# First layer's hand-over from cross attention to the experts: the last batch in other PSUM banks, the next norm begun in the block before it, and the experts' weights for tiles 1 and 2 handled sooner

## The reference

```
def _L0_xattn_ref(hs, at, mask, Wq, bq, Wk, bk, Wv, bv, Wo, bo, ln_gamma, ln_beta, residual_scale):
    ...                                             # 16 heads of 16, over 256 keys
    scores = clip(einsum('bhsd,bhtd->bhst', q, k) / sqrt(16), -50, 50)
    probs = softmax(where(attend, scores, -50), axis=-1)
    ctx = einsum('bhst,bhtd->bhsd', probs, v)
    delta = clip(residual_scale, 0, 0.3) * (ctx @ Wo.T + bo)
    return layernorm(delta) * ln_gamma + ln_beta

def _moe_forward(x, router_weight, gate_up_proj, down_proj, sh_gate_w, sh_up_w, sh_down_w, shared_gate_w):
    shared = silu(x @ sh_gate_w.T) * (x @ sh_up_w.T) @ sh_down_w
    combine = top2_of_8(softmax(x @ router_weight.T))
    for e in range(8):
        gate, up = split(x @ gate_up_proj[e].T)
        out = out + (silu(gate) * up @ down_proj[e].T) * combine[:, e:e + 1]
    return out + sigmoid(x @ shared_gate_w.T) * shared

x = x + _L0_xattn_ref(_layernorm(x), ctx_2048, mask, ...)
x = x + _moe_forward(_layernorm(x), ...)
```

## Time and profile before

| | |
|---|---|
| median of 3 runs | 1137.29 us (1137.09 to 1137.39) |
| the profiled execution's own time | 1135.79 us |
| its span, first to last instruction | 1134.0 us |
| PE busy | 1014.3 us (89%), mean granted clock 0.959 |
| DVE busy | 748.9 us (66%) |
| ACT busy | 628.8 us (55%) |
| POOL busy | 402.7 us (36%) |
| DMA | 53.62 MB, mean 47 GB/s |
| the tail of the cross attention, from its last scores to the barrier | 421.9 to 444.8 us of the span |
| the experts' block up to the first matmul of tile 2 | 444.8 to 487.8 us |

### The profile page before, as it was taken

The page is one execution under the profiler, slowest core; times in us unless marked ns, Lnnn a source line. Parts: engine busy times, 40 slices in busy tenths (PEclk is TensorE's granted clock), DMA queues, the critical chain, the costliest instruction groups (busy, mean ns, idle before and its releaser), DMA issues. The chain is left out here.

```text
span 1134.0 us, 21031 instructions
## 1 busy us (share of the span) xinstructions
PE 1014.3 (89%) x7004; PEld 821.8 (72%) x7004; DVE 748.9 (66%) x2168; ACT 628.8 (55%) x1557; POOL 402.7 (36%) x381
## 2 busy tenths in 40 slices
PE   5799999999997984889998589999999997879978
PEld 4567777777764553778887368888888885767868
DVE  6667777777654576355655757777777775557984
ACT  2167777777773771233432557777777764334323
POOL 6466666666643012000000544443434331110150
PEclk9999999999999997799999699999999998988999
DMA  4250222111005000254441000001101000000111
GB/s 151 70 179 19 57 48 57 38 30 39 2 1 213 1 2 1 59 122 113 100 115 37 5 29 27 26 28 32 37 14 37 24 10 1 1 1 29 44 40 52
DMA packets 27242, 53.62 MB, mean 47 GB/s; under 512 B 4546, under 2 KB 11778, under 8 KB 26782
## 3 DMA queue, kind: packets, MB, share of 16 engines
q1 hardware_dynamic: 27166, 52.65, 16.9%
HBM read 42.56 MB, written 1.69 MB: 39 GB/s over the span
## 5 line engine op out<-in xcount | busy, mean ns | idle before, releaser
L387 POOL TENSOR_TENSOR sb_a_P<-sb_a_P,sb_a_rec 128x512 f32<-128x512 f32 x128 | 130.2, 1040 | 109.0 <-DVE sb_a_rec L592 109.0
L469 ACT ACTIVATE sb_a_P<-sb_a_nS,sb_a_nm 128x257 f32<-128x257 f32 x256 | 128.2, 508 | 19.7 <-DVE sb_a_nm L581 19.4
L581 DVE CUSTOM_DVE_ANT_0 sb_a_nS<-a_pS,sb_a_mask,sb_a_nsink 128x256 f32<-128x256 f32 x256 | 107.7, 480 | 42.1 <-PE a_pS L705 42.1
L478 ACT COPY sb_xn<-a_pT 128x512 f32<-128x512 f32 x128 | 74.9, 585 | 85.3 <-PE a_pT L719 84.6
L1785 ACT ACTIVATE sb_a_t<-a_pp,sb_a_w 64x512 f32<-64x512 f32 x128 | 87.4, 683 | 21.5 <-PE a_pp L142 17.1
L142 PE MATMUL a_pp<-sb_x_high,sb_a_w_low 128*128 128x512 f32 x188 | 83.4, 444 | 7.9 <-DVE sb_a_P L536 2.5
L719 PE MATMUL a_pT<-sb_ident,sb_a_P 128*128 128x128 f32 x512 | 82.0, 283 | 4.1 <-ACT sb_xn L478 4.1
L142 PE MATMUL a_pY<-sb_a_wo_high,sb_a_OT_low 128*128 128x256 f32 x256 | 74.7, 292 | 11.5 <-DVE sb_a_OT_low L135 9.4
L1858 DVE SCALAR_TENSOR_TENSOR sb_a_t<-a_pp,sb_a_w,sb_a_cs 128x512 f32<-128x512 f32 x64 | 47.8, 748 | 55.6 <-ACT sb_a_t L1785 55.5
L719 PEld LDWEIGHTS a_pT<-sb_ident,sb_a_P 128*128 128x128 f32 x512 | 55.3, 141 | 39.6 <-issue 32.4
L1716 POOL TENSOR_TENSOR sb_a_qT<-sb_a_t 128x512 f32<-128x512 f32 x32 | 41.1, 1286 | 117.4 <-DVE sb_a_t L1861 117.4
(11 more groups left out here) (374 smaller groups left out, 3056.7 us busy)
## 6 DMA issues: line engine op xcount, KB each, us to landing
sb_m_cw<-m_table SPq DMA_DIRECT2D x15, 512.0 KB
sb_a_kr<-sb_a_kall SPq DMA_DIRECT2D x56, 128.0 KB, 2.4
sb_f_w<-f_w SPq DMA_DIRECT2D x12, 384.0 KB, 3.1
sb_m_gu<-m_gu SPq DMA_DIRECT2D x17, 256.0 KB, 6.5
sb_a_w<-a_w SPq DMA_DIRECT2D x16, 257.0 KB, 2.7
sb_m_dn<-m_dn SPq DMA_DIRECT2D x17, 128.0 KB, 6.6
sb_a_w<-a_w SPq DMA_DIRECT2D x8, 259.0 KB, 2.6
sb_a_wo<-a_wo SPq DMA_DIRECT2D x8, 256.0 KB, 2.9
```

The costliest lines, as they stand in the source:

```text
L387: nc.gpsimd.tensor_tensor(part, part, rec[b % 2][:, h, :].rearrange("p (q o) -> p q o", o=1) .to_broadcast([P, 2, S]), ALU.mult).then_inc( ...
L469: out = nc.scalar.activation(Pm[b % 2][:, h, qt, 0:S + 1], nS[:, h, qt, 0:S + 1], ACT.Exp, bias=nm[b % 2][:, h, qt:qt + 1], scale=-1.0, ac ...
L478: nc.scalar.copy(PT[h], pT[:, :]).then_inc(PT_ready, 1)
L581: out = nc.vector.tensor_tensor_reduce(nS[:, h, qt, 0:S], pS[h][:, qt * S:(qt + 1) * S], wmask[:, qt, :], -1.0, nsink[par][:, h:h + 1], AL ...
```

## The change

Four things. (1) In the cross attention the last batch's tail uses banks of `pS`, which hold no more scores by then, in place of `pc`: its two halves have banks of their own, so that each half is transposed, copied and projected after its own semaphore (`turnedO`, `OT_ready`, `projected` count each half), and `turn_oT(3)` waits for the last exponential in place of `scaled`. (2) DVE does `add_normed(2)` at n = 37, behind `normalise(3, 0)` and `(3, 1)`. (3) The norm of the experts' input begins in the cross attention's block: DVE takes the statistics of tiles 0 to 3 at n = 28 and scales them at n = 31, with POOL's inverse root between `root(1)` and `root(2)`; the statistics of tiles 4 to 7 are DVE's last work before the barrier; in the experts' block POOL's root and DVE's scaling remain for the second half only. (4) In the experts' block ACT and DVE split the gate-up weights of tile 1 right behind the norm, in place of in step 0, and SP waits for the table inside its step, behind the request for gate-up weights.

```diff
@@ class BegunNorm
-        self.ln, self.rstd_ready, self.xn_ready = (k.sem(f"{tag}_{name}") for name in ("ln", "rstd_ready", "xn_ready"))
+        sem = lambda name: k.nc.alloc_semaphore(name=f"{tag}_{name}")
+        self.ln, self.rstd_ready, self.xn_ready = sem("ln"), sem("rstd_ready"), sem("xn_ready")
@@ cross_attention_0
+        following = k.norm_of_m0
+        LAST = B - 1
+        def bank_of_turned(b, qt):
+            return front[qt] if b == LAST else pc
+        def bank_of_O(b, qt):
+            return (front[2], pS[2][:, 0:NC])[qt] if b == LAST else pc
+        def bank_of_out(b, qt):
+            return half_of((front[3], pS[2][:, NC:2 * NC])[qt] if b == LAST else pc, qt)
@@ gpsimd
+            pool.sem_inc(following.rstd_ready, 1)
             for b in range(B):
                 root(b)
+                if b == 1:
+                    inverse_root(nc, pool, k, following.ln, following.rstd_ready, 0, halves=(0,))
@@ scalar, evac_OT
-                nc.scalar.copy(OT[:, :, :, :].rearrange("p t c q -> p (t c q)"), pc[:, :]).then_inc(OT_ready, 1)
+                if b < LAST:
+                    nc.scalar.copy(OT[:, :, :, :].rearrange("p t c q -> p (t c q)"), pc[:, :]).then_inc(OT_ready, 1)
+                    return
+                for qt in range(2):
+                    act.wait_ge(turnedO, b + 1 + qt)
+                    nc.scalar.copy(OT[:, qt, :, :].rearrange("p c q -> p (c q)"), half_of(bank_of_O(b, qt), qt)).then_inc(OT_ready, 1)
@@ vector
-                o = pc[:, :].rearrange("p (h n) -> p h n", h=X0_H)
+                o = bank_of_turned(b, qt)[:, :].rearrange("p (h n) -> p h n", h=X0_H)
...
-                    out = nc.vector.scalar_tensor_tensor(out=delta[:, 2 * b + qt, :], in0=half_of(pc, qt),
+                    if b == LAST:
+                        dve.wait_ge(projected, b + 1 + qt)
+                    out = nc.vector.scalar_tensor_tensor(out=delta[:, 2 * b + qt, :], in0=bank_of_out(b, qt),
...
-                    if n == 8 * b + 18:
+                    if n == 8 * b + 18 and b != LAST - 1 or n == 8 * b + 21 and b == LAST - 1:
                         add_normed(b)
+                if n == 28:
+                    dve.wait_ge(summed, HALF)
+                    row_stats(nc, dve, k, k.x, following.ln, 0, 0)
+                if n == 31:
+                    row_scale(nc, dve, k, k.x, k.xn, following.rstd_ready, 0, 0, following.xn_ready)
             dve.wait_ge(summed, NT)
+            row_stats(nc, dve, k, k.x, following.ln, 0, 1)
+            dve.wait_ge(following.ln, 4 * HALF)
@@ tensor, turn_oT
-                    else:
+                    elif b < LAST:
                         pe.wait_ge(scaled, b)
-                else:
+                    if b == LAST:
+                        pe.wait_ge(probs, X0_PAIRS)
+                elif b < LAST:
                     pe.wait_ge(O_ready, 2 * b + 1)
...
@@ tensor, turn_O and project_out
-                pe.wait_ge(O_ready, 2 * b + 2)
+                pe.wait_ge(O_ready, 2 * b + (1 if b == LAST else 2))
                 for qt in range(2):
+                    if b == LAST and qt == 1:
+                        pe.wait_ge(O_ready, 2 * b + 2)
...
+                    if b == LAST and qt == 0:
+                        out.then_inc(turnedO, 1)
                 out.then_inc(turnedO, 1)
...
+                    if b == LAST and qt == 1:
+                        pe.wait_ge(OT_ready, b + 2)
...
+                    if b == LAST and qt == 0:
+                        out.then_inc(projected, 1)
                 out.then_inc(projected, 1)
@@ experts_0
-            norm_and_turn(nc, k, ctx, "m0", [pg[0], pg[1], pu[0], pu[1]], split=True)
+            norm_and_turn(nc, k, ctx, "m0", [pg[0], pg[1], pu[0], pu[1]], split=True, begun=k.norm_of_m0)
@@ sync
                 sp.wait_ge(h_ready, 2 * n + 2)
+                sp.wait_ge(table_out, 16)
                 weights_of(n + 2, par)
...
-            sp.wait_ge(table_out, 16)
             with sp.Fori(0, PAIRS) as i:
@@ scalar
             gate_up_high(0, 0)
             on_scalar(act)
+            gate_up_high(1, 1)
             act.wait_ge(gates, 1)
...
-                if not (isinstance(n, int) and n == LAST):
+                if not (isinstance(n, int) and n in (0, LAST)):
                     gate_up_high(n + 1, 1 - par)
@@ vector
             gate_up_low(0, 0)
             lows_on_vector(dve)
+            gate_up_low(1, 1)
...
-                if not (isinstance(n, int) and n == LAST):
+                if not (isinstance(n, int) and n in (0, LAST)):
                     gate_up_low(n + 1, 1 - par)
@@ program
+        k.norm_of_m0 = BegunNorm(k, "m0")
         cross_attention_0(nc, k, src)
```

More of the change, by code:

```diff
@@ L1177, in turn_oT @@
                         pe.wait_ge(q_out, b + 3)
-                    else:
+                    elif b < LAST:
                         pe.wait_ge(scaled, b)
-                else:
+                    if b == LAST:
+                        pe.wait_ge(probs, X0_PAIRS)
+                elif b < LAST:
                     pe.wait_ge(O_ready, 2 * b + 1)
                 for q in range(X0_QUADS):
-                    out = nc.tensor.transpose(pc[:, q * P:(q + 1) * P],
+                    out = nc.tensor.transpose(bank_of_turned(b, qt)[:, q * P:(q + 1) * P],
                                               oT[q // 2][:, (q % 2) * S + qt * P:(q % 2) * S + (qt + 1) * P],
@@ L1188, in turn_O @@
             def turn_O(b):
-                pe.wait_ge(O_ready, 2 * b + 2)
+                pe.wait_ge(O_ready, 2 * b + (1 if b == LAST else 2))
                 for qt in range(2):
+                    if b == LAST and qt == 1:
+                        pe.wait_ge(O_ready, 2 * b + 2)
                     for c in range(KD):
-                        out = nc.tensor.transpose(pc[:, (2 * qt + c) * P:(2 * qt + c + 1) * P],
+                        out = nc.tensor.transpose(bank_of_O(b, qt)[:, (2 * qt + c) * P:(2 * qt + c + 1) * P],
                                                   O[qt][:, c * 8:(c + 1) * 8, :].rearrange("p h n -> p (h n)"),
                                                   k.tile["ident"][:, :])
+                    if b == LAST and qt == 0:
+                        out.then_inc(turnedO, 1)
                 out.then_inc(turnedO, 1)
@@ L1199, in project_out @@
                 for qt in range(2):
+                    if b == LAST and qt == 1:
+                        pe.wait_ge(OT_ready, b + 2)
                     for c in range(KD):
-                        out = nc.tensor.matmul(half_of(pc, qt), OT[:, qt, c, :], w[:, 3, c, :],
+                        out = nc.tensor.matmul(bank_of_out(b, qt), OT[:, qt, c, :], w[:, 3, c, :],
                                                start=(c == 0), stop=(c == KD - 1))
+                    if b == LAST and qt == 0:
+                        out.then_inc(projected, 1)
                 out.then_inc(projected, 1)
```

## The result

The changed kernel takes 1126.93 us (median of 7 runs, 1124.09 to 1131.36) beside 1137.29 us of the kernel before on the same chip (7 runs, 1136.42 to 1138.94): a ratio of 0.9911, 95% interval 0.989 to 0.9932. The prediction was 1128.2 us with a range of 1123.8 to 1131.8, and faster with a chance of 0.93. The profiled execution took 1124.25 us (before: 1135.79).

What follows compares the result with a forecast made beforehand. PE was taken as the bound, so only its waits or half-clock time pay: 6.7 (router) - 0.6 (clock) + 2.2 (request) + 0.8 (tile 2's clock) = 9.1 us, giving 1128.2 us, range 1123.8 to 1131.8.

Steps and rivals of the forecast that it cites:

- The tail: End of the cross attention, batch 3: its projection ends at 435.4 against 439.85, 4.45 us sooner.
- the case of full clock throughout: Batch 3's projection with no fall of PE's clock: ends at 434.5, router 7.6 us sooner.
- with the clock falling where it fell: Assumption for batch 3's projection: PE's clock falls at about 433.5 as before, so it ends at 435.4.
- The price of the half norm: Cross attention: statistics begun early delay PE's weighing by 0.15 us, bounds 0 and 1.7.
- The clock at the head: Experts' router and gate_up(0): the low-clock stretch may be up to twice 3.1 us; 0.6 us of loss taken.
- Tile 2's request: Experts' loop entry: tile 2's weights, requested right behind the table, land 2.2 us sooner, bounds 0.3 and 3.9.
- The rival of data that overtake the table: Tile 2's weights come in while the table is still being written: gain 12.3 us, 1125.0 us; chance 0.2.
- PE's idle time before tile 2: Sign in the experts' block: PE's idle time, 3.93 us before, would be under 3 us.
- the 0.8 us that I had credited to tile 2: Less idle time before tile 2 saves half of the 1.7 us lost there to PE's low clock.
- The hand-over alone: Rival: the request comes no sooner or the clock takes it back; gain 5.5 us, 1131.8 us; chance 0.13.
- the half norm on the path: Rival: clips move by 1.7 us, scalings by 1.35, projection at half clock; gain 5.2 us, 1132.1 us; chance 0.05.
- the slower loop: Rival: experts' loop tiles wait for data, at 1.0 us a tile over 14 tiles 1142.2 us; chance 0.03.

Runs made afterwards that it cites:

- the banks alone: The kernel before with only the last batch's own banks and the moved addition of batch 2: 1130.01 us beside 1137.75, ratio 0.9922.
- the addition back: The changed kernel with batch 2's addition again ahead of batch 3's divisions: 1129.11 us beside 1141.35, ratio 0.9903.
- the profile of after: First profiled execution of the changed kernel, set against the single profile of the kernel before: 1124.25 us beside 1135.79.
- the second profile: The unaltered changed kernel, timed and profiled again beside the version with early requests: 1128.25 us beside 1138.3 for the kernel before, ratio 0.9899.
- the request alone: The kernel before with only SP's table wait moved behind the gate-up request and tile 1's sooner split: 1136.53 us, ratio 0.9978.
- the wait back: The changed kernel with SP's wait for the table ahead of the experts' loop again: 1127.89 us, ratio 0.9884 to the kernel before.
- the kept-warm kernel: The changed kernel with tiles 2 and 3 requested at the experts' head, plus six and ten unused matmuls around the norm: 1122.65 us beside 1141.35, ratio 0.9835.
- with six: The kernel with early requests and unused matmuls, plus 6 of gate_up(0)'s matmuls between the router's: 1119.78 us beside 1138.3, ratio 0.982.
- with twelve: The kernel with early requests and unused matmuls, plus 12 of gate_up(0)'s matmuls between the router's: 1120.78 us, ratio 0.9841.

## Why the prediction was right

**The tail.** The working put the end of the projection at 435.4, the clock falling at 433.5; the case of full clock throughout was 434.5. In the profile the projection is taken up 20.20 us behind the landmark, or 434.46: the clock held, and the 7.6 us of that case are the 7.57 measured at the router. The step that was mis-sized is "with the clock falling where it fell". Before, PE waited 2.71, 0.81 and 0.67 us ahead of the last groups of the tail, and the clock fell at about 433.5; now the waits are 0.71, 0.78 and 0.18 us and the clock is at 1.00 up to 442. This is no chance of one execution: the projection took 1.99 us in all eleven profiles of kernels with the new banks, that of the banks alone (its end at 20.08) among them, and 3.78 us in all three with the old ones. One long wait is not what does it: with the addition back PE waits 2.27 us in one piece, and the clock holds. Which part of the old chain let it fall is open. The price of the half norm was 0.15 us predicted and some 0.1 measured.

**The clock at the head.** Predicted at +0.6 us, it was -1.5 in the profile of after and +1.1 in the second profile of the same kernel. The low stretch in `gate_up(0)`, 3.1 us before and allowed up to twice that, was 3.6 and 5.2 us. What the working did not have is that the router itself can begin at full clock, as it did in the profile of after. The guess was inside the spread by luck, and its sign is not a property of the change.

**Tile 2's request.** 2.2 us predicted; 2.36 in the change, 2.33 for the request alone, 2.45 given back with the wait. The rival of data that overtake the table falls: they came 8.5 us behind their request (8.6 predicted), and only asked for ahead of the table were they early. The Trainium skill ("DMA: Bandwidth & Descriptors", Two DMAs through the same engine are not ordered) says that a later descriptor can complete before an earlier one has written; no run here shows it for these two requests on one queue. The table's completion, put at some 1 us behind its data, fits the run with the wait back: the data are through at about 477, and the request that waits for them goes out at 478.02.

**The signs.** In the times of before (less 4.20 us) the barrier came at 440.8 (441 to 442.5 predicted), the router's first matmul at 446.7 (447 to 448.5) and the request of tile 2's weights at 465.9 (about 469): all three sooner than said, the first two by the tail's clock, the third by the clock at the head as well; in the second profile the request came at 468.6. The cast stood 8.5 us behind the request (8.6), DVE's last clip did not move, and the loop had no idle time of PE.

**PE's idle time before tile 2** is the sign that came out longer than said in the profile of after (3.54 against under 3). I had left `gate_up(1)` and `down(0)` as slow as before. At a faster clock PE reached the same landing sooner and waited longer, so the speed turned into idle time, and of the 0.8 us that I had credited to tile 2 only 0.20 were measured. In the second profile the idle time is 1.05 and the row of tile 2 to 3 gives 1.33. The two terms of the clock together were predicted at 0.8 - 0.6 = 0.2 us of gain; they were 1.7 us in the first profile and 0.2 in the second. Two profiles of one kernel differ by more than the term.

**The other rivals.** The hand-over alone (5.5 us) falls by the request's 2.3 us; the half norm on the path falls by the clips; the slower loop falls by 126.84 us in place of 126.87. That nothing outside these chains holds the router or the barrier falls by the 7.57 us. That tile 1's split is hidden was shown by putting it back.

**The sum.** Local gains of 11.6 and 9.9 us in the two profiles of the changed kernel bracket its medians, 10.4 and 10.05 us under before, against 9.1 predicted: the term of the tail was 0.9 short, and the rest, as far as the rows show, is the clock's. Both local gains are counted against the same single profile of before, so that they bracket the medians is a check and not a proof.

## What to carry to other kernels

Where one queue writes a result and then fetches weights, moving the fetch up to the write gained here only the gap between the write's last data and the fetch's first (2.3 to 2.5 us, the write's completion and the start of the fetch); moving it ahead of the write gained the rest, 4.7 us in the medians and 1.7 or 4.7 in the two pairs of profiles. A step ahead of a join is worth what the other side leaves: PE's idle time was 3.54 or 1.05 us by its own speed, for the same landing. And where runs of one kernel spread over 7 us, count landmarks from an instruction ahead of the edit, and take two profiles, before a microsecond is put down to a part.

## What the runs showed of the hardware that was not expected

- PE busy in every nanosecond did not hold the clock: while it did the router's matmuls of 9 columns the clock fell from 1.00 (0.98) to 0.50, in the changed and in the kept-warm kernel, PE busy 3.00 of 3.00 and 2.00 of 2.00 us. With six or twelve matmuls of 512 columns between them it was 1.00 through the router, in one profile of each.
- Where the clock was gained at the router, it was lower in the next product: 1.6 us won up to the transposes, 1.5 lost up to tile 2. Whether the one brings the other stays open, and so does why the clock fell right behind the router with six (PE busy 2.00 of 2.00 us before it) and not with twelve.
- The same code took 12.44 or 15.04 us from the router to the transposes in two executions, and nothing in the rows but the clock differs.
- On one queue data followed their request in 8.5 us behind a table (changed kernel, 470.14 to 478.63) and in 2.7 us when the table had landed (wait back, 478.02 to 480.70).
